# A decoder block on one core: SyncE's transfers listed when their input is ready, and the last row's x kept in its tile

## What is computed

```python
x = _layernorm(x + _L0_attn_ref(x, ...))              # two Mamba layers
x = _layernorm(x + _L0_xattn_ref(ctx_1024, ctx_1024, x, ...))
x = _layernorm(x + _L0_ffn_ref(x, ...))               # 8 experts, the best 2 per position
# one Mamba layer, in its core:
def step(h, inp):
    u_t, dt_t, B_t, C_t = inp
    dA = jnp.exp(dt_t[:, :, None] * A)
    h = h * dA + (dt_t * u_t)[:, :, None] * B_t[:, None, :]
    y = jnp.einsum('bds,bs->bd', h, C_t)
    return (h, y)
# experts: softmax over 8 logits, top 2 renormed, and
h = jax.nn.relu(jnp.einsum('td,ehd->teh', xf, w1) + b1)   # 1024 hidden
expert_out = jnp.einsum('teh,edh->ted', h, w2) + b2
```

## Time and profile before

| | us |
|---|---|
| median of three runs | 3226.01 |
| lowest, highest | 3223.88, 3228.01 |
| profiled execution | 3228.65 |
| its span, first to last instruction | 3226.9 |
| mean granted TensorE clock, of full speed | 0.974 |
| VectorE busy in the span | 2880.8 |
| TensorE busy in the span | 2857.8 |

### The profile page before, as it was taken

One profiled execution on the slowest core, in us unless ns is written; L12 is line 12 of the kernel. 1 busy time (PEld: TensorE's weight loads), 2 busy tenths in 40 slices (PEclk: granted clock), 3 DMA queues, 4 the chain that ended last, 5 costly groups with the idle time before them and its releaser, 6 DMA issues.

```text
span 3226.9 us, 59765 instructions
## 1 busy us (share of the span) xinstructions
PE 2857.8 (89%) x21930; PEld 2612.9 (81%) x21930; DVE 2880.8 (89%) x2005; ACT 2629.2 (81%) x6114; POOL 2660.8 (82%) x1317
## 2 busy tenths in 40 slices
PE   6889899998888899897999999889898998999876
PEld 5888888886777788786888888878787887988776
DVE  6999999999999999998999999999999999999510
ACT  7878888886978888896899889898897988988422
POOL 4989999898989899897998888887988988977421
PEclk8999999999999999998999999999999999999988
DMA  3345422222222222222332443423223453534286
GB/s 109 100 166 169 144 71 64 71 74 71 65 67 66 69 69 65 64 74 85 91 113 93 129 138 117 122 83 120 91 85 111 145 161 103 158 121 127 94 298 211
DMA packets 294567, 352.73 MB, mean 109 GB/s; under 512 B 106346, under 2 KB 191603, under 8 KB 293892
## 3 DMA queue, kind: packets, MB, share of 16 engines
q1 hardware_dynamic: 290322, 338.14, 33.9%
q0 software_dynamic: 3072, 8.39, 0.7%
q10 hardware_dynamic: 882, 2.38, 0.2%
HBM read 306.45 MB, written 42.36 MB: 108 GB/s over the span
## 4 chain that ended last, share of the span: by engine, by line
PE 33%; ACT 20%; DVE 19%; POOL 12%; issue 12%; DMA 2%; SPq 1%; POOLq 0%; DVEq 0%; ACTq 0%
DVE h L1366 13%; POOL hC L1121 10%; ACT dA L1334 10%; PE psY L1679 8%; PE psX L1660 8%; PE psG L1618 6%; DVE psX L1356 4%; ACT xs L1305 3%; PE psX L1650 3%; PE psG L1705 3%; PE psX L1618 2%; ACT gT L1176 1%; DMA w_up<-in_w_exp 1%; PE psX L1642 1%; POOL scratch L1041 1%
## 5 line engine op out<-in xcount | busy, mean ns | idle before, releaser
L1121 POOL TENSOR_TENSOR hC<-h,cb 128x1024 f32<-128x1024 f32 x1024 | 2401.6, 2369 | 372.8 <-DVE h L1366 334.0
L1366 DVE TENSOR_TENSOR_SCAN h<-dA,psX 128x1024 f32<-128x1024 f32 (+1 forms) x1097 | 2304.5, 2134 | 121.4 <-ACT dA L1334 46.9
L1334 ACT ACTIVATE dA<-dt,negA 128x255 f32<-128x255 f32 x4096 | 1720.1, 505 | 131.8 <-DVE h L1366 129.8
L1679 PE MATMUL psY<-ident,hC 128*128 128x128 f32 x8192 | 1074.5, 275 | 9.8 <-POOL hC L1121 9.1
L1679 PEld LDWEIGHTS psY<-ident,hC 128*128 128x128 f32 x8192 | 937.2, 142 | 18.5 <-POOL hC L1121 17.5
L1660 PE MATMUL psX<-diag_b,dtuT 128*128 128x128 f32 x4416 | 566.9, 283 | 84.6 <-DVE h L1366 76.5
L1660 PEld LDWEIGHTS psX<-diag_b,dtuT 128*128 128x128 f32 x4416 | 533.0, 196 | 128.8 <-issue 120.2
L1650 PE MATMUL psX<-ident,xs 128*128 128x128 f32 x2928 | 392.0, 278 | 111.0 <-ACT xs L1305 77.4
L1305 ACT ACTIVATE xs<-dtuT,bT 128x512 f32<-128x512 f32 x732 | 487.4, 719 | 2.5 <-PE psX L1650 2.4
L1356 DVE TENSOR_TENSOR psX<-dtu,psX 128x1024 f32<-128x1024 f32 x382 | 461.9, 1209 | 16.7 <-PE psX L1642 16.4
L1650 PEld LDWEIGHTS psX<-ident,xs 128*128 128x128 f32 x2928 | 331.5, 142 | 164.4 <-ACT xs L1305 101.6
(11 more groups left out here) (219 smaller groups left out, 2048.3 us busy)
## 6 DMA issues: line engine op xcount, KB each, us to landing
cb<-c_dram SPq DMA_DIRECT2D x256, 512.0 KB
w_up<-in_w_exp SPq DMA_DIRECT2D x170, 256.0 KB
w_down<-in_w_exp SPq DMA_DIRECT2D x170, 256.0 KB
diag_b<-b_dram SPq DMA_DIRECT2D x276, 128.0 KB
x_slots<-got SPq DMA_DIRECT2D x24, 512.0 KB, 4.9
y_slots<-got SPq DMA_DIRECT2D x24, 512.0 KB, 5.0
dA<-in_w_exp SPq DMA_DIRECT2D x42, 256.0 KB, 4.7
h<-in_w_exp SPq DMA_DIRECT2D x42, 256.0 KB
```

Of the source, the lines that this page charges most:

```text
L1121: eng.tensor_tensor(hC[i % NHC][:, :, :], h[i % NH][:, :, :], cw.to_broadcast([P, KI, L]), ALU.mult).then_inc(times_c, 1)
L1334: made = eng.activation(dA[j % NA][:, c, 1:L], dt[n % 2][:, c, 1:L], ACT.Exp, scale=negA[:, JOBS[n][0], c, s:s + 1])
L1366: made = eng.tensor_tensor_scan(h[i % NH][:, part, :].rearrange("p c t -> p (c t)"), dA[i % NA][:, part, :].rearrange("p c t -> p (c t)"), ...
L1679: made = eng.matmul(psY[:, tc, c * P:(c + 1) * P], hC[i % NHC][:, c, tc * P:(tc + 1) * P], ident[:, :], start=s == 0 and c == 0, stop=s == ...
```

## The change

Two things. The last row (7) has no `spill` and no `acc_load`: its x stays in the tile `x2`, which no later row needs, and `blend`, the normalization and the store work on `x2`. And a transfer's limit in the planner is now about when its input is ready, not when it would have landed: it is placed when that time is at least 3 us (`SETTLED`) before the planned end of the next scan, where before it might be up to 10 us less its length after it. The store of C (`c_store`) and the load of the next row's x (`row_in`) become pieces of their own. `resid1` now needs `row_in`. Since users are placed behind their transfers, the places of other pieces move with them.

```diff
+SETTLED = 3000
             task("c_copy", n, 0, "ACT", 400, ("c+", n, 0), frees=("c", n, 0)),
+            task("c_store", n, 0, "DMA", 2500, ("c_copy", n, 0)),
-                task("resid1", b, 0, "DVE", 2350, ("proj+", b, 1), frees=("proj", b, 0)),
+                task("resid1", b, 0, "DVE", 2350, ("proj+", b, 1), *((("row_in", b, 0),) if b else ()), frees=("proj", b, 0)),
     then("norm2", 0, scaler(b), 780, *((("spill", b - 1, 0),) if b > 0 else ()))
+    if b < ROWS - 1:
+        out.append(task("row_in", b + 1, 0, "DMA", 3000, ("norm2", b, 0)))
-    out.append(task("spill", b, 0, "DMA", 3000, ("b2_add", b, 0)))
+    if b < ROWS - 1:
+        out.append(task("spill", b, 0, "DMA", 3000, ("b2_add", b, 0)))
-        out.append(task("acc_load", b, 0, "DMA", 3000, ("spill", b, 0), *((("stored", b - 1, 0),) if b and not alone else ())))
+        if not alone:
+            out.append(task("acc_load", b, 0, "DMA", 3000, ("spill", b, 0), *((("stored", b - 1, 0),) if b else ())))
-        out += [task("blend", b, tc, "DVE", 970, ("fetched", b, 0), ("acc_load", b, 0)) for tc in range(KL)]
+        out += [task("blend", b, tc, "DVE", 970, ("fetched", b, 0), ("b2_add" if alone else "acc_load", b, 0)) for tc in range(KL)]
-                    if at + t.ns <= limit[t.eng] + over:
+                    if (at if t.eng == "DMA" else at + t.ns) <= limit[t.eng] + over:
-                limit["DMA"] = then + 10000
+                limit["DMA"] = then - SETTLED
-        acc_of = {b: homes[ROWS - 1 - b] if b in plan.late_rows else acc[:, :, :] for b in range(ROWS)}
+        acc_of = {b: homes[ROWS - 1 - b] if b in plan.late_rows else acc[:, :, :] for b in range(ROWS - 1)}
+        acc_of[ROWS - 1] = x2[:, :, :]
-                    if name == "c_copy":
+                    if name == "c_store":
-                    elif name == "norm2" and n + 1 < ROWS:
-                        on.wait_ge(normed[1], n + 1)
-                        eng.dma_start(xrow[:, :, :], io["x"][n + 1]).then_inc(xrow_in, 16)
+                    elif name == "row_in":
+                        on.wait_ge(normed[1], n)
+                        eng.dma_start(xrow[:, :, :], io["x"][n]).then_inc(xrow_in, 16)
-                        on.wait_ge(acc_in[n], 16)
+                        if n < ROWS - 1:
+                            on.wait_ge(acc_in[n], 16)
```

## The result

| | before | changed |
|---|---|---|
| median, us (8 runs of each, one chip) | 3224.7 | 3234.56 |
| lowest, highest | 3218.75, 3236.52 | 3229.12, 3239.48 |
| ratio, 95% interval | | 1.0028, 1.0017 to 1.0039 |
| profiled execution, its span | 3228.65, 3226.9 | 3232.81, 3230.9 |

The forecast was 3219.0 us, faster; the time lies above its range. A second comparison, on another chip, gave 1.0037 [1.0024, 1.005]. The two profiled executions lie on opposite sides of their medians, so their spans differ by 4.0 us where the medians differ by 9.9.

What follows compares the result with a forecast made beforehand. VectorE's scans were taken to bound the loop, TensorE with the experts the end. Loop -9.1, behind it +3.2, freer engines -1.1 gave -7.0 us: 3226.0 to 3219.0, own range 3214 to 3224, eight in ten 3208 to 3231.

Steps and rivals of the forecast that it cites:

- Part 1: In the loop, SyncE no longer held before unready transfers: 6.8 us gone near 1519, 2.3 at a second place, 9.1 in all.
- The second place: At 2692.41 us a kept row's load delays two w_down loads; of VectorE's 2.90 us wait, 2.3 taken as gone.
- the 14.9 us of the earlier trace: TensorE's waits for weights, ten pieces; eight have SyncE waiting for a quarter in use, said to stay unchanged.
- Part 2: Later listing's price in the loop: 1.5 us less VectorE waiting for weights, against 1.5 us for late x of tiles.
- the class in the earlier trace: VectorE's loop stalls for ScalarE's late decays, 46.9 us; fewer expert pieces there were taken to save 1.1 us.
- Part 3: Behind the loop, six tiles left: 31.0 us more TensorE work, less 27.4 holes and 5.9 clock, plus 3.5 and 2.0: +3.2 us.
- the holes for xg: Behind the loop, TensorE's idle 8.20 us until the first xg and 7.66 before 3103.25, counted as room for moved tiles.
- the hole of 7.66: TensorE's wait before 3103.25 us, as x was stored and reloaded ahead of tile 40's rows; keeping x removes that.
- (a): Rival: behind the loop six tiles don't fit the holes, +8 to +11 us cancels the loop's 9; 3226, chance 0.22.
- (b): Rival: all VectorE time lost to weights and matrices and the ScalarE share go, tail at 0; 3208.5, chance 0.13.
- (c): Rival: in the loop TensorE waits for late x of tiles, 2.3 us each; about 3234, 3239 at worst, chance 0.12.
- (d): Rival: 3 us of settling may leave SyncE standing; only the place near 1519 might move; 3224 to 3228, chance 0.11.

Runs made afterwards that it cites:

- own rows: Changed kernel, but tiles 38 and 39 each load their own rows at their own place; 3224.69 us, ratio 0.9992 to the kernel before.
- list moved: Changed kernel with tile 38's load, which also fetches tile 39's rows, listed behind tile 36's store; 3231.81 us, ratio 1.0005 to the kernel before.
- experiment 2: Two kernels: the changed one without `row_in`, 3216.25 us, ratio 0.9958; the kernel before with only `row_in` added, 3241.19 us, ratio 1.0046.
- x spilled: Changed kernel, but row 7's x is stored and loaded back as before; ratio 1.001 to the kernel before.

## Why the prediction was wrong, step by step

**Part 1, the place at 1519: right.** Taken as 6.8 us; job 8 is 7.0 shorter, in every kernel that lists the tile late, and not with x kept alone or `row_in` alone (184.8, 185.2). The second place, 2.3 us at 2698: that wait is gone, and of the 14.9 us of the earlier trace rows these are left in the loop (total us, times, longest), but jobs 9 to 15 didn't get shorter by it:

```profile
PE psG L1626 <- DMA w_up<-in_w_exp: 4.0, 4, 2.2
PE psG L1713 <- DMA w_down<-in_w_exp: 0.2, 1, 0.2
```

**Part 2, the price in the loop: mis-sized, and its cause wrong.** Jobs 9 to 15 were to give 2.3 + 1.5 - 1.5, and 1.1 of the class in the earlier trace rows: 3.4 us in all. They came out 1 to 4 us longer than in the kernel before. The waits for ScalarE's decays did fall a little from 1700 us on, from 23.2 to 20.2 us. Those for TensorE's filling of `psX` shifted between its three ways, and in sum rose from 27.7 to 28.9 us. Of VectorE in the changed kernel, and then in the kernel before, 1700 to 3015 us:

```profile
DVE h L1373 <- ACT dA L1341: 20.2, 24, 3.1
DVE h L1373 <- PE psX L1668: 16.2, 17, 1.8
DVE h L1373 <- PE psX L1658: 7.8, 7, 2.2
...
DVE psX L1363 <- PE psX L1650: 4.9, 8, 2.0
```

```profile
DVE h L1366 <- ACT dA L1334: 23.2, 28, 3.1
DVE psX L1356 <- PE psX L1642: 12.8, 13, 3.3
DVE h L1366 <- PE psX L1660: 9.1, 12, 1.5
DVE h L1366 <- PE psX L1650: 5.8, 5, 2.9
```

So the moved pieces changed which engine is last, for nothing in sum. One thing went against the prediction's idea that fewer expert pieces leave TensorE freer. It has 218 fewer products in jobs 9 to 15, which at 7.24 us a tile is an estimated 33 us of its time, but its busy time there fell by only 9 to 16 us (1232.9 and 1237.2 before, 1224.1 and 1221.3 changed). Its mean granted clock over these jobs is 0.97 in both executions of the changed kernel and 0.99 and 0.98 in those of before. Whether this lower clock ate the gain was not tested; own rows and list moved, with the same list of the loop, have 0.98 there. A difference of 1 to 4 us is within what executions of one kernel differ by, so only "no gain" is shown, not a loss. The step "its users are planned behind it, so the expert pipeline turns more slowly" named the wrong cause of the six tiles: it was `row_in` (experiment 2). I had read what moved and given it to the larger edit, without parting the edits.

**Part 3, the stretch behind the loop: the step that failed.** Its sum was +3.2 us, its upper end +11; it measured +7.6, and against the second execution of before +5.5. (The upper end was itself added up too low: with only the holes for xg filled and half the clock regained, the terms give 31.0 - 15.9 - 3.0 = 12.1, and 17.6 with the last two.) The sum can be laid beside TensorE's busy and idle time in the stretch. Busy was to grow by 31.0 - 5.9 = 25.1 us and grew by 23.0 (153.4 to 176.4). Idle was to fall by 27.4 - 3.5 - 2.0 = 21.9 and fell by 15.4 (56.3 to 40.9). With own rows it falls by 23.6. So the work was sized well, and the missing term is the new hole. The terms for which rows stood were too cautious: all listed holes were filled, the clock stayed at full speed from 3030 to the hole, TensorE waited some 0.53 us at a turning (0.7 was taken), and the 2.0 us left for the row's chain weren't needed. With the hole out of the way the stretch is 208.6 us (own rows), 1.1 less than in the first execution of before, or 211.6 (list moved), 1.9 more. What failed is a sentence of one line: "The store and the load are gone, and nothing else there waits." The sum priced the moved tiles on TensorE and ScalarE alone. Their entries on SyncE, stores through one `yg` and a combined load with two waits, were moved to behind the loop too, and I didn't lay them beside the list of the last group. The move had to be priced on SyncE's queue as well, where Part 1 had found the same pattern: a transfer that isn't ready, listed ahead of one that is.

**Keeping x: right in mechanism, void in this order.** Alone it took 5.1 us off the hole of 7.66 and 6.2 off the stretch. In the changed kernel six tiles cover that hole, so the same 7.66 us had been counted as room for the tiles; that was consistent, but the edit itself then earns nothing. This fits the changed kernel standing 0.70 to 0.79% above the one without `row_in` by their ratios, more than the 0.46% of that piece alone: the piece also takes back what keeping x had brought.

**The rivals.** (a) comes nearest, the tail takes the gain, with the right size (8 to 11 us) and the wrong place: its test, TensorE idle for over 8 us in the last row's chain, was met over 20 us after the chain's last product. Its sum still gave 3226, for it credited the loop with 9 us, of which only the 7 of job 8 came. (b) asked for stalls beyond job 8 to go at no cost behind the loop, and neither came. (c), the slower one, did not occur: TensorE never waited for `xg` in the loop. That the time lies in (c)'s part of the range is chance. (d) was right in part: SyncE still stands in the loop (34.5 us before the next x), and job 8 alone gained; it foresaw no hole behind the loop. The rule of the Trainium skill to issue a DMA early (DMA: Bandwidth & Descriptors, section Rules for kernel authors) spoke for (c). The trace agrees with it at one place, tile 36's store, which was ready at 3077.3 and issued at 3088.34; what made it late was its place in the list.

**The numbers.** By the table, second executions included, the change is -6.9 (job 8), +1 to +4 (jobs 9 to 15), +5.5 to +8.5 (behind the loop), the last two with means of +2.5 and +7.0: +2.6 us. The ratios say +9 to +12. Jobs 0 to 7, where the two executions of a kernel differ by 2.4 to 4.2 us in sum, have +2.2 of the rest on the mean; one profiled execution need not lie at the median either. So 4 to 7 us of the slowdown are located nowhere. Against the forecast of -7.0 the loop came out 5.8 us short (-10.2 with the 1.1 of decays, -4.4 measured), and the stretch behind it 3.8 us too long (+3.2 and +7.0).

## What to carry over

A transfer with two waits, or one that isn't ready, held all that SyncE had listed behind it, 15.3 us from 1488.93 on in the kernel before and 7.5 us from 3075.71 on in the changed one. So before work is moved, write down for each single buffer which store frees it, and what stands ahead of that store in the issuing engine's list. A change made of several edits is priced edit by edit, each with its own order; here the edit that looked like bookkeeping moved four and a half tiles. A hole that is filled by other work can't be claimed a second time by the edit that would have closed it.

## What was not expected of the hardware

Job 8 begins at different times in one kernel's executions, by 2.4 us (before: 1485.1 and 1487.5) and 4.2 us (changed: 1486.4 and 1490.6), as much as several edits here move; job 8 repeats to 0.3 us. One such difference could be read. With one and the same list of the loop, job 10 took 184.5 us in both executions of the changed kernel, 182.6 with x spilled, and 181.2 in the ones with own rows and with the list moved. Its windows, first of the changed kernel, then of the one with own rows (columns as above):

```profile
1857.00:2041.00 184.00, 169.29 (x1313) 156.69 (x1313) 174.63 (x94) 163.65 (x385) 164.45 (x79) 0.98 0.39 121
```

```profile
1857.00:2038.00 181.00, 166.63 (x1315) 153.83 (x1316) 174.85 (x94) 163.66 (x386) 164.72 (x79) 1.00 0.39 123
```

The same work is done in 3 us less, with TensorE's mean clock at 1.00 where it was 0.98 and 2.7 us less busy time on it. In the changed kernel the granted clock is 0.50 (1.2 GHz) in two stretches of that job, from 1972.7 and from 2003.4 us, at the same places of the job in its second execution. With x spilled there is one such stretch, and with own rows or the list moved none. Each one made the job some 1.5 us longer, though TensorE was busy for 92% of it, so in this loop little of such a fall is hidden from VectorE. Ahead of the first one TensorE had waited 2.22 us for `xs`; it waits as long at the same place with own rows, and the clock does not fall there. What lets it fall in one execution and not in the next, the traces don't show.
